# Transformer layer on eight cores: softmax division after the row sum moved behind a DRAM broadcast, weight casts issued one step ahead

## The chip, the cores and the metric

One Trainium2 chip. The same program runs on all 8 of its cores, each with its own rows of the result; the cores do not talk to each other. The metric is the device time in microseconds (us) of the slowest core. Engines are named as in the profile: PE is TensorE (matmul), PEld its weight loads, DVE is VectorE, ACT is ScalarE, POOL is GpSimd, SP is SyncE, which here only issues DMAs.

## The reference, cut to what matters

```python
# x: (2, 4096, 2048), float32
def attn(x):                       # 32 heads of 64 features
    q, k, v = x @ Wq + bq, x @ Wk + bk, x @ Wv + bv
    scores = einsum('bdsh,bdth->bdst', q, k) / sqrt(32)
    weights = softmax(scores, axis=-1)
    feats = einsum('bdst,bdth->bdsh', weights, v)
    return feats @ Wo + bo
def ffn(x):                        # hidden size 5632, integer weights
    return qlinear(silu(qlinear(x, wq_gate)) * qlinear(x, wq_up), wq_down)
x = x + attn(layernorm(x))
x = x + ffn(layernorm(x))
```

## The kernel before, in words

Core c takes batch c//4 and 1024 of its 4096 rows as queries; it computes K and V for all 4096 rows itself. Every step of the program is appended to one list with its engine, the semaphore counts it waits for and the one it raises (`st`, L173). Each engine then executes its own steps strictly in the order of the list, with no scheduler behind it. So the place of a step in the list is its place in its engine's queue, and a step that waits holds up all behind it on the same engine.

The stages, in order of time:

- **Projection** (L262 to L419), in two halves of 2048 rows. LayerNorm first (L263 to L314). Then for `w` in k, v (and q in the first half) and for each of 16 blocks `fo` of 128 output features: SP loads 1 MB of float32 weights into `wst` (L332, two buffers), ACT casts them to bf16 in `wbf` (L337, two buffers), PE does 64 matmuls of 128x512 (32 for q, L349), and ACT evacuates PSUM to `kev` or `qT` (L365, two evacuations, one for q). For k and q, ACT squares the result (L375, L413), and PE and DVE take turns over it in `_norms` (L233) to find a bound on the scores. For v, PE transposes `kev` in two groups of eight (L386), ACT copies each group to `vts` (L393), and POOL issues four DMAs to `vslab` in DRAM (L407). In ACT's queue the cast of block `fo` stands behind all the ACT work of block `fo-1`, and the first matmul of block `fo` waits for that cast.
- **Attention** (L467 to L582), 16 pairs of two heads, `p` and `h2`, head number `d = 2p + h2`. The K and V of a pair come by SP DMAs (`prefetch`, L488), issued two pairs ahead, when the last PE step of a pair is over. V has an extra column of ones, so row 64 of the result in PSUM is the softmax's row sum. A head has 32 chunks `c` of 128 keys. For each, PE computes the scores (two matmuls, L523, PSUM banks 0,1 or 2,3 in turn), ACT takes the exponential into `pt` (L540, 1024 columns), and PE multiplies by V (two matmuls, L551) and accumulates in banks 4,5 (h2=0) or 6,7 (h2=1). The scores of chunk c+2 are issued just ahead of the V product of chunk c.
- **End of a head** (L559 to L573): DVE takes the reciprocal of row 64, 1024 numbers in one partition, into `rcd`; PE copies it to 64 partitions by multiplying it with a column of ones (`ones64`, L563), into banks 2,3, the banks which chunk 1 of the next head needs; ACT copies that to `ebc` (L568); DVE multiplies the head's result by it and writes `featsT` (L570). The scores of chunk 0 of the next head stand behind the multiplication by ones in PE's queue; those of chunk 1 also wait for ACT's copy (`prev_eb`).
- **Output projection** (L586 to L631): a bias load on POOL and eight DVE additions that need it, then 512 matmuls.
- **FFN** (L636 to L790): 44 blocks of gate and up matmuls, and a down projection after every group of eight.

Of the kernel before, what the change touches and what calls it, by code (L numbers as in the profile page):

```python
# [6 lines left out]
F32 = mybir.dt.float32  # L7
# [3 lines left out]
ALU = mybir.AluOpType  # L11
# [21 lines left out]
def build(stop_after=99, debug=False, sub=99):  # L33
    nc = bass.Bass("TRN2", target_bir_lowering=False)
# [42 lines left out]

    identb = alloc("identb", [128, 128], BF16)
    identf = alloc("identf", [128, 128], F32)
    ones64 = alloc("ones64", [128, 64], F32)  # L80
    biasB = alloc("biasB", [128, NH], F32)
    bqs = alloc("bqs", [128, 16], F32)
    bks = alloc("bks", [128, 16], F32)
# [15 lines left out]
    lds2 = alloc("lds2", [128, 128], F32)  # L99
    P_END = off[0]  # L100
    assert P_END - PB <= 4096, P_END - PB
    R1 = PB + 4096
    R2 = R1 + 32768
    R3 = R2 + 32768
    SB_LIMIT = 229376
# [4 lines left out]
    featsT = alloc("featsT", [128, 16 * TO], BF16, at=R2)  # L110
# [16 lines left out]
          alloc("va1", [128, 32 * 2 * 128], BF16, at=FL + 49152)]  # L127
    pt = [alloc("pt0", [128, TO], BF16, at=FL + 65536),
          alloc("pt1", [128, TO], BF16, at=FL + 67584)]
    ebc = alloc("ebc", [128, TO], F32, at=FL + 69632)  # L130
    rcd = ebc[64:65, 0:TO]
    owst = alloc("owst", [128, 16 * 512], F32, at=FL)
    owbf = [alloc("owbf0", [128, 16 * 512], BF16, at=FL + 32768),
            alloc("owbf1", [128, 16 * 512], BF16, at=FL + 49152)]
# [12 lines left out]
    wdbB = alloc("wdbB", [128, 4 * D], BF16, at=FL + 49152)  # L147
    sdb = alloc("sdb", [128, D], F32, at=FL + 65536)
    gsil = alloc("gsil", [128, TO], BF16, at=FL + 73728)
    assert FL + 75776 <= SB_LIMIT  # L150

    PSA = nc.alloc_psum_tensor("PSA", [128, 4096], F32)

# [31 lines left out]

    for t_, val in ((identb[:, :], 0.0), (identf[:, :], 0.0), (ones64[:, :], 1.0),
                    (kmax[:, :], 0.0), (qmax[:, :], 0.0),
                    (epst[:, :], EPS), (n128[:, :], -128.0),
                    (ldst[:, :], 0.0), (lds2[:, :], 0.0)):
        st("gpsimd", lambda g, tt=t_, val=val: g.memset(tt, val), inc=gS)  # L190
# [70 lines left out]
    if stop_after >= 1:  # L261
        for h in (range(2) if sub >= 11 else []):  # L262
# [64 lines left out]
            for iw, w in enumerate(ws):  # L327
                wt, bcol, wscale = Wmap[w]
                ntq = 1 if w == "q" else 2
                for fo in range(16):  # L330
                    pg = cast_g.get((iw, fo - 2), cast_g.get((iw - 1, 14 + fo), 0))
                    ldw = st("sync", lambda e, wt=wt, fo=fo: e.dma_start(  # L332
                        out=wst[fo % 2].ap().rearrange("p (c x) -> p c x", x=128),
# [4 lines left out]
                        out=wbf[fo % 2][:, :], in_=wst[fo % 2][:, :]),  # L338
                        waits=[(dWp[fo % 2], ldw), (tS, mmg), (sS, sS.n)], inc=sS)
                    cast_g[(iw, fo)] = cg  # L340
                    for tq in range(ntq):
                        pb = 0 if tq == 0 else 2
                        ev_p = evac_g.get((iw, fo - 1, tq),
                                          evac_g.get((iw - 1, 15, tq), 0))
                        for fi in range(16):
                            for nh in range(2):
                                mvw = lnxT[:, fi * 2048 + tq * 1024 + nh * 512:
                                           fi * 2048 + tq * 1024 + (nh + 1) * 512]
                                st("tensor", lambda t, pb=pb, nh=nh, fo=fo, fi=fi, mvw=mvw: t.matmul(  # L349
                                    bkf(pb + nh), wbf[fo % 2][:, fi * 128:(fi + 1) * 128],  # L350
                                    mvw, start=(fi == 0), stop=(fi == 15)),
                                    waits=([(sS, cg), (vS, ln_done), (sS, ev_p)]
                                           if fi == 0 and nh == 0 else []),
                                    inc=tS if (fi == 15 and nh == 1) else None)
# [14 lines left out]
                        evac_g[(iw, fo, tq)] = ev  # L369
# [97 lines left out]
    if stop_after >= 2:  # L467
# [38 lines left out]
        prefetch(0)  # L506
        prefetch(1)
        fn_guard = {}
        prev_exp30 = 0
        prev_eb = 0  # L510
        prev_av = None
        for p in range(NP):
            need_dF = 160 * (p // 2 + 1)
            for h2 in range(2):
# [19 lines left out]
                for c in range(32):  # L534
# [21 lines left out]
                            waits=avw2 if qh == 0 else [],  # L556
                            inc=tS if qh == 1 else None)
                    av_cnt[c] = tS.n
                rc = st("vector", lambda v, acb=acb: v.reciprocal(  # L559
                    out=rcd, in_=PSA[64:65, acb * 512:(acb + 2) * 512]),  # L560
                    waits=[(tS, av_cnt[31]), (vS, vS.n)], inc=vS)
                for qh in range(2):
                    st("tensor", lambda t, qh=qh: t.matmul(  # L563
                        PSA[0:64, (2 + qh) * 512:(3 + qh) * 512], ones64[64:65, 0:64],
                        rcd[:, qh * 512:(qh + 1) * 512], start=True, stop=True),
                        waits=[(vS, rc), (sS, exp_cnt[31])] if qh == 0 else [],
                        inc=tS if qh == 1 else None)
                eb = st("scalar", lambda s: s.copy(out=ebc[0:64, :], in_=PSA[0:64, 1024:2048]),  # L568
                        waits=[(tS, tS.n), (sS, sS.n)], inc=sS)
                fg = st("vector", lambda v, p=p, h2=h2, acb=acb: v.tensor_tensor(  # L570
                    out=featsT[h2 * 64:(h2 + 1) * 64, p * 1024:(p + 1) * 1024],
                    in0=PSA[0:64, acb * 512:(acb + 2) * 512], in1=ebc[0:64, :],
                    op=ALU.mult), waits=[(sS, eb), (vS, vS.n)], inc=vS)  # L573
                fn_guard[(p + 1, h2)] = fg
                prev_exp30 = exp_cnt[30]
                prev_eb = eb
                prev_av = av_cnt
                if h2 == 1:
                    pair_end[p] = tS.n
# [310 lines left out]
```

How the kernel before makes its waits and increments, by code:

```python
def build(stop_after=99, debug=False, sub=99):  # L33
# [787 lines left out]
               waits=[(dB, S["dB"].n)], inc=dO, k=16)  # L821
        if stop_after >= 2 and stop_after < 4:
            st("sync", lambda e: e.dma_start(out=dbg["f"].ap(), in_=featsT[:, :]), inc=dO, k=16)
        if stop_after >= 3:
            for i in range(8):
                st("sync", lambda e, i=i: e.dma_start(
                    out=dbg["r1"][i * 128:(i + 1) * 128, :], in_=res[:, i * D:(i + 1) * D]),
                   inc=dO, k=16)
    final = dO.n
    st("sync", lambda e: e.wait_ge(dO.h, final))
    with nc.Block() as blk:
        for ename in ENGS:
# [1 line left out]
                def body(e):  # L836
                    for (en, fn, waits, incs) in steps:
                        if en != ename:
                            continue
                        for (h, v) in waits:
                            e.wait_ge(h, v)
                        inst = fn(e)
                        for (s_, k_) in incs:
                            inst.then_inc(s_.h, k_)
```

## Time and profile before

| what | value |
|---|---|
| median of the 2 runs of before | 5039.8 us (4981.63 and 5097.97) |
| the profiled execution: its time | 5000.85 us |
| its span, slowest core (7) | 4999.3 us |
| spans of all cores | 4968.2 to 4999.3 us |
| mean granted TensorE clock | 0.854 to 0.861 |
| PE busy | 3645.9 us (73%) |
| ACT busy | 1949.0 us (39%) |
| DVE busy | 910.3 us (18%) |
| POOL busy | 164.5 us (3%) |

The span runs from the first to the last instruction of the slowest core. The granted clock is a share of full speed: 1.00 is 2.4 GHz and 0.50 is 1.2 GHz. A row of the timeline reads: start in us, duration in us (of a whole group where several instructions are merged), engine, line, operation, output<-inputs, and in square brackets how long the engine had been idle before it and whose end released it. SPq and POOLq rows are the issue of DMAs, not their transfer.

### The profile page before, as it was taken

The page shows a single profiled execution, that of the slowest core. Times are in us where ns is not written, and L with a number is a line of the kernel's source. Part 1 is how long each engine was busy: PE and PEld are TensorE (multiplying, and loading weights), DVE is VectorE, ACT ScalarE, POOL GpSimd, SP SyncE. Part 2 cuts the span into 40 slices and gives each one's busy share as a digit, 9 for nine tenths or more (in the row PEclk, how much of TensorE's full clock was granted, in tenths as well). Part 3 has the DMA queues.
Part 4 walks back from the last instruction along what each step waited for, and adds up shares of the span by engine and source line. Part 5 has one row for each costly group of instructions (what it writes and reads, how often), then busy time and mean ns, then how long its engine had stood idle before and what let it go on. Part 6 is the DMA issues. An engine that isn't in the chain of part 4 may idle for free.

```text
span 4999.3 us, 44517 instructions; the slowest of 8 cores (4968.2 to 4999.3 us)
## 1 busy us (share of the span) xinstructions
PE 3645.9 (73%) x15365; PEld 1448.1 (29%) x15365; DVE 910.3 (18%) x1172; ACT 1949.0 (39%) x1658; POOL 164.5 (3%) x190
## 2 busy tenths in 40 slices
PE   2676677674466777747777777777775879999997
PEld 1232333221222333312222222222221334444443
DVE  4211000013311100001111111111112232223223
ACT  3222222223222222237677676767765231232121
POOL 0000011100000011120000000000000000000000
PEclk9877888876677788879888888888887979999999
DMA  3211222222211122240010001100011343453343
GB/s 127 76 59 64 63 64 64 72 72 88 102 63 63 51 64 65 57 105 17 17 34 17 17 17 28 24 17 17 17 17 72 114 142 122 149 202 127 125 153 127
DMA packets 257363, 361.58 MB, mean 72 GB/s; under 512 B 140578, under 2 KB 140672, under 8 KB 243072
## 3 DMA queue, kind: packets, MB, share of 16 engines
q1 hardware_dynamic: 245888, 322.99, 21.4%
q0 software_dynamic: 11264, 35.75, 2.3%
q8 instruction: 136, 2.23, 0.2%
q14 instruction: 75, 0.61, 0.0%
HBM read 316.76 MB, written 41.94 MB: 72 GB/s over the span
## 4 chain that ended last, share of the span: by engine, by line
PE 62%; ACT 18%; DVE 10%; issue 6%; DMA 2%; POOL 1%; ACTq 0%; DVEq 0%; SPq 0%; POOLq 0%
PE PSA L349 24%; ACT pt L540 11%; PE PSA L523 7%; PE PSA L773 6%; PE PSA L731 6%; PE PSA L741 6%; PE PSA L551 5%; DVE ebc L559 4%; PE PSA L563 2%; PE PSA L617 2%; PE PSA L237 2%; DVE scr L244 2%; ACT kev L365 1%; ACT vts L393 1%; ACT sqst L375 1%
## 5 line engine op out<-in xcount | busy, mean ns | idle before, releaser
L349 PE MATMUL PSA<-lnxT,wbf 128*128 128x512 bf16 x4608 | 1187.0, 425 | 112.0 <-ACT wbf L337 110.5
L540 ACT ACTIVATE pt<-PSA,biasB 128x1024 bf16<-128x1024 f32 x1024 | 1102.4, 1112 | 193.8 <-PE PSA L551 120.2
L523 PE MATMUL PSA<-qT,kp 128*128 128x512 bf16 x2048 | 652.9, 402 | 226.2 <-ACT pt L540 148.1
L349 PEld LDWEIGHTS PSA<-lnxT,wbf 128*128 128x128 bf16 x4608 | 490.1, 107 | 777.7 <-issue 375.7
L551 PE MATMUL PSA<-pt,va 128*128 128x512 bf16 x2048 | 623.9, 387 | 24.5 <-ACT pt L540 24.0
L559 DVE RECIPROCAL ebc<-PSA 1x1024 f32<-1x1024 f32 x32 | 209.8, 6555 | 1282.3 <-PE PSA L551 1282.3
L523 PEld LDWEIGHTS PSA<-qT,kp 128*128 128x128 bf16 x2048 | 135.7, 97 | 762.1 <-issue 761.7
L244 DVE TENSOR_REDUCE scr<-PSA 128x8 f32<-128x512 bf16 x160 | 110.7, 692 | 1278.6 <-PE PSA L237 1278.6
L237 PE MATMUL PSA<-identb,sqst 128*128 128x128 bf16 x640 | 87.1, 283 | 335.9 <-DVE kmax L252 149.5
L365 ACT ACTIVATE kev<-PSA,bks 128x1024 bf16<-128x1024 f32 x64 | 71.3, 1114 | 656.7 <-PE PSA L349 656.7
L731 PE MATMUL PSA<-ln2xT,wgb 128*128 128x512 bf16 x1408 | 313.0, 381 | 2.9 <-ACT wgb L709 2.9
L741 PE MATMUL PSA<-ln2xT,wub 128*128 128x512 bf16 x1408 | 311.1, 379 | 0.0
L551 PEld LDWEIGHTS PSA<-pt,va 128*128 128x128 bf16 x2048 | 196.8, 98 | 297.3 <-issue 81.6
L563 PE MATMUL PSA<-ebc,ones 1*64 1x512 f32 x128 | 116.5, 1062 | 223.4 <-DVE ebc L559 223.4
L365 ACT ACTIVATE kev<-PSA,bvs 128x1024 bf16<-128x1024 f32 x64 | 71.3, 1114 | 504.7 <-PE PSA L349 430.6
L749 ACT ACTIVATE gsil<-PSA,sgc 128x1024 bf16<-128x1024 f32 x44 | 49.0, 1114 | 503.6 <-PE PSA L731 503.5
L301 PE MATMUL PSA<-identb,lnst 128*128 128x128 bf16 x512 | 70.8, 302 | 200.1 <-ACT lnst L290 187.1
L773 PE MATMUL PSA<-wdbA,gub 128*128 128x512 bf16 x768 | 180.4, 381 | 11.8 <-DVE gub L755 11.8
L731 PEld LDWEIGHTS PSA<-ln2xT,wgb 128*128 128x128 bf16 x1408 | 138.2, 98 | 170.5 <-issue 5.6
L741 PEld LDWEIGHTS PSA<-ln2xT,wub 128*128 128x128 bf16 x1408 | 137.8, 98 | 166.2
L568 ACT COPY ebc<-PSA 64x1024 f32<-64x1024 f32 x32 | 32.2, 1006 | 368.4 <-PE PSA L563 368.4
L237 PEld LDWEIGHTS PSA<-identb,sqst 128*128 128x128 bf16 x640 | 51.9, 120 | 383.3 <-issue 383.3
(100 smaller groups left out, 2003.0 us busy)
## 6 DMA issues: line engine op xcount, KB each, us to landing
wdi<-wd SPq DMA_DIRECT2D x44, 1024.0 KB, 5.0
xst<-xb SPq DMA_DIRECT2D x32, 1024.0 KB, 5.3
kslab<-kev POOLq DMA_DIRECT2D x32, 512.0 KB, 2.9
vslab<-vts POOLq DMA_DIRECT2D x128, 128.0 KB, 4.4
kp<-kslab SPq DMA_DIRECT2D x32, 512.0 KB, 6.6
va<-vslab SPq DMA_DIRECT2D x128, 128.0 KB, 3.2
owst<-wo SPq DMA_DIRECT2D x4, 4096.0 KB, 13.8
res<-xb SPq DMA_DIRECT2D x8, 1024.0 KB, 19.4
```

What stands on the lines that cost most here:

```text
L237: st("tensor", lambda t, b4=b4, j=j, bank=bank, sqtile=sqtile: t.transpose(bkb(bank)[:, j * 128:(j + 1) * 128], sqtile[:, (b4 * 4 + j) * 1 ...
L244: st("vector", lambda v, bank=bank: v.reduce_sum(out=scr.ap().rearrange("p (a b) -> p a b", b=2)[:, 0:4, :], in_=bkb(bank)[:, 0:512].rearr ...
L349: st("tensor", lambda t, pb=pb, nh=nh, fo=fo, fi=fi, mvw=mvw: t.matmul(bkf(pb + nh), wbf[fo % 2][:, fi * 128:(fi + 1) * 128], mvw, start=( ...
L365: wscale=wscale: s.activation(out=dst, in_=bkf(pb, 2), func=AF.Identity, bias=bcol[:, fo:fo + 1], scale=wscale),
L523: st("tensor", lambda t, p=p, h2=h2, c=c, qh=qh: t.matmul(bkf((0 if c % 2 == 0 else 2) + qh), kp[p % 2][:, h2 * TB + c * 128: h2 * TB + (c ...
L540: e = st("scalar", lambda s, p=p, c=c, d=d: s.activation(out=pt[c % 2][:, :], in_=bkf(0 if c % 2 == 0 else 2, 2), func=AF.Exp, bias=biasB[ ...
L551: st("tensor", lambda t, p=p, h2=h2, c=c, qh=qh, acb=acb: t.matmul(PSA[:, (acb + qh) * 512:(acb + qh + 1) * 512], vav[p % 2][:, c, h2, 0:128],
L559: rc = st("vector", lambda v, acb=acb: v.reciprocal(out=rcd, in_=PSA[64:65, acb * 512:(acb + 2) * 512]), waits=[(tS, av_cnt[31]), (vS, vS. ...
L563: st("tensor", lambda t, qh=qh: t.matmul(PSA[0:64, (2 + qh) * 512:(3 + qh) * 512], ones64[64:65, 0:64], rcd[:, qh * 512:(qh + 1) * 512], s ...
L731: st("tensor", lambda t, fi=fi, nh=nh, hc=hc: t.matmul(bkf(nh), wgb[:, fi * 128:(fi + 1) * 128], ln2xT[:, fi * 1024 + nh * 512: fi * 1024 ...
L741: st("tensor", lambda t, fi=fi, nh=nh, hc=hc: t.matmul(bkf(2 + nh), wub[:, fi * 128:(fi + 1) * 128], ln2xT[:, fi * 1024 + nh * 512: fi * 1 ...
L773: wdbuf=wdbuf, wslot=wslot, last=(jj == len(grp) - 1): t.matmul(bkf(pb + nh), gub[:, jj * 1024 + qt * 128:jj * 1024 + (qt + 1) * 128], wdb ...
```

## The change

Two edits, and a third that follows from them.

**Casts.** Load and cast of a weight block become a helper, `ldcast`. It is called for block 0 before the loop, and inside the loop for block `fo+1` ahead of the matmuls of block `fo` (for block 0 of the next matrix when `fo` is 15).

**End of a head.** The reciprocal no longer reads PSUM, and PE no longer broadcasts. ACT copies row 64 to partition 0 of `nbc` (`dsb`), DVE copies the undivided result to `featsT` in bf16 and takes the reciprocal in place, POOL writes the 1024 reciprocals to DRAM (`dslab`) and reads them back to 64 partitions of `nbc`, and DVE multiplies `featsT` in SBUF. The next head's chunk 1 waits only for the last exponential.

**Memory.** `ones64` and its memset are gone, and the big buffers begin right behind the small ones: 512 bytes lower in each partition than before.

```diff
-    R1 = PB + 4096
+    R1 = ((P_END + 63) // 64) * 64
...
+                def ldcast(iw, fo, wt):
                     pg = cast_g.get((iw, fo - 2), cast_g.get((iw - 1, 14 + fo), 0))
                     ldw = st("sync", lambda e, wt=wt, fo=fo: e.dma_start(
...
                     cast_g[(iw, fo)] = cg
+
+                if (iw, 0) not in cast_g:
+                    ldcast(iw, 0, wt)
+                for fo in range(16):
+                    if fo + 1 < 16:
+                        ldcast(iw, fo + 1, wt)
+                    elif iw + 1 < len(ws):
+                        ldcast(iw + 1, 0, Wmap[ws[iw + 1]][0])
+                    cg = cast_g[(iw, fo)]
...
-                rc = st("vector", lambda v, acb=acb: v.reciprocal(
-                    out=rcd, in_=PSA[64:65, acb * 512:(acb + 2) * 512]),
+                cd = st("scalar", lambda s, acb=acb: s.copy(
+                    out=dsb, in_=PSA[64:65, acb * 512:(acb + 2) * 512]),
+                    waits=[(tS, av_cnt[31]), (sS, sS.n), (vS, nrm_g.get(d - 1, 0)),
+                           (dR, rsb_dma.get(d - 1, 0))],
+                    inc=sS)
+                fg = st("vector", ... v.tensor_copy(
+                    out=featsT[h2 * 64:(h2 + 1) * 64, p * 1024:(p + 1) * 1024],
+                    in_=PSA[0:64, acb * 512:(acb + 2) * 512]),
                     waits=[(tS, av_cnt[31]), (vS, vS.n)], inc=vS)
-                for qh in range(2):
-                    st("tensor", lambda t, qh=qh: t.matmul(
-                        PSA[0:64, (2 + qh) * 512:(3 + qh) * 512], ones64[64:65, 0:64],
-                        rcd[:, qh * 512:(qh + 1) * 512], start=True, stop=True),
-                        waits=[(vS, rc), (sS, exp_cnt[31])] if qh == 0 else [],
-                        inc=tS if qh == 1 else None)
-                eb = st("scalar", lambda s: s.copy(out=ebc[0:64, :], in_=PSA[0:64, 1024:2048]),
-                        waits=[(tS, tS.n), (sS, sS.n)], inc=sS)
-                fg = st("vector", lambda v, p=p, h2=h2, acb=acb: v.tensor_tensor(
+                fn_guard[(p + 1, h2)] = fg
+                rc = st("vector", lambda v: v.reciprocal(out=rsb, in_=dsb),
+                        waits=[(sS, cd), (vS, vS.n), (dR, rsb_dma.get(d - 1, 0))], inc=vS)
+                st("gpsimd", lambda g, d=d: g.dma_start(
+                    out=dslab[d].unsqueeze(0), in_=rsb),
+                    waits=[(vS, rc)], inc=dR, k=16)
+                rsb_dma[d] = dR.n
+                st("gpsimd", lambda g, d=d, h2=h2: g.dma_start(
+                    out=nbc[0][h2 * 64:(h2 + 1) * 64, :],
+                    in_=dslab[d].unsqueeze(0).partition_broadcast(64)),
+                    waits=[(dR, dR.n), (vS, nrm_g.get(d - 1, 0))], inc=dR, k=16)
+                ng_ = st("vector", ... v.tensor_tensor(
                     out=featsT[h2 * 64:(h2 + 1) * 64, p * 1024:(p + 1) * 1024],
-                    in0=PSA[0:64, acb * 512:(acb + 2) * 512], in1=ebc[0:64, :],
-                    op=ALU.mult), waits=[(sS, eb), (vS, vS.n)], inc=vS)
-                fn_guard[(p + 1, h2)] = fg
+                    in0=featsT[h2 * 64:(h2 + 1) * 64, p * 1024:(p + 1) * 1024],
+                    in1=nbc[0][h2 * 64:(h2 + 1) * 64, :], op=ALU.mult),
+                    waits=[(dR, bcd), (vS, fg), (vS, vS.n)], inc=vS)
+                nrm_g[d] = ng_
...
-                prev_eb = eb
+                prev_eb = exp_cnt[31]
```

How the instructions stand on the engines. ACT's queue at the start of the projection, before (L337 is the cast, L365 the evacuations of a block, L375 the square):

```order
L290 ACTIVATE lnst<-xst_70,negmr,rstd 128x2048
L337 CAST wbf_73<-wst_71 128x2048
L365 ACTIVATE kev<-PSA,bks 128x1024 x2
L375 ACTIVATE sqst<-kev 128x2048
L337 CAST wbf_74<-wst_72 128x2048
L365 ACTIVATE kev<-PSA,bks 128x1024 x2
```

The same place after (L339, L376 and L386 are the same three steps):

```order
L291 ACTIVATE lnst<-xst_69,negmr,rstd 128x2048
L339 CAST wbf_72<-wst_70 128x2048
L339 CAST wbf_73<-wst_71 128x2048
L376 ACTIVATE kev<-PSA,bks 128x1024 x2
L386 ACTIVATE sqst<-kev 128x2048
L339 CAST wbf_72<-wst_70 128x2048
L376 ACTIVATE kev<-PSA,bks 128x1024 x2
```

A second cast stands ahead of the first evacuation. From there on the pattern of the queue is the old one, but each cast belongs to the block after the one whose matmuls come next.

PE's queue around the end of head 0, before (L523 scores, L551 products with V, L563 the multiplication by ones):

```order
L551 MATMUL PSA<-pt_84,va_81 128x512 x2
L551 MATMUL PSA<-pt_83,va_81 128x512 x2
L551 MATMUL PSA<-pt_84,va_81 128x512 x2
L563 MATMUL PSA<-ebc,ones_45 64x512 x2
L523 MATMUL PSA<-qT,kp_79 128x512 x6
L551 MATMUL PSA<-pt_83,va_81 128x512 x2
```

PE's queue there after (L537 scores, L565 products with V):

```order
L565 MATMUL PSA<-pt_83,va_80 128x512 x2
L565 MATMUL PSA<-pt_82,va_80 128x512 x2
L565 MATMUL PSA<-pt_83,va_80 128x512 x2
L537 MATMUL PSA<-qT,kp_78 128x512 x6
L565 MATMUL PSA<-pt_82,va_80 128x512 x2
```

The next head's scores now follow the last product with V directly. ACT's queue there, after (L554 the exponential, L573 the copy of the row sum), has the copy where the copy from banks 2,3 (L568) stood:

```order
L554 ACTIVATE pt_82<-PSA,biasB 128x1024
L554 ACTIVATE pt_83<-PSA,biasB 128x1024
L573 COPY nbc_84<-PSA 1x1024
L554 ACTIVATE pt_82<-PSA,biasB 128x1024
```

DVE's queue per head, after, is three instructions (before: L559 reciprocal and L570 product):

```order
L580 CAST featsT<-PSA 64x1024
L585 RECIPROCAL nbc_84<-nbc_84 1x1024
L597 TENSOR_TENSOR featsT<-featsT,nbc_84 64x1024
```

and POOL's, which had nothing in this stage after its memsets:

```order
L588 DMA dslab<-nbc_84 16x1x64
L592 DMA nbc_84<-dslab 64x1024
```

## Rows read from the trace of the kernel before

**Rows 1.** The page's chain of work that ended last, by engine and by line

```profile
PE 62%; ACT 18%; DVE 10%; issue 6%; DMA 2%; POOL 1%; ACTq 0%; DVEq 0%; SPq 0%; POOLq 0%
PE PSA L349 24%; ACT pt L540 11%; PE PSA L523 7%; PE PSA L773 6%; PE PSA L731 6%; PE PSA L741 6%; PE PSA L551 5%; DVE ebc L559 4%; PE PSA L563 2%; PE PSA L617 2%; PE PSA L237 2%; DVE scr L244 2%; ACT kev L365 1%; ACT vts L393 1%; ACT sqst L375 1%
```

**Rows 2.** Who waited for whom: total us, times, longest us

```profile
DVE ebc L559 <- PE PSA L551: 1282.3, 32, 95.1
...
PE PSA L563 <- DVE ebc L559: 223.4, 32, 7.0
...
PE PSA L349 <- ACT wbf L337: 110.5, 31, 3.8
```

**Rows 3.** Timeline, the end of one head and the start of the next

```profile
3003.26 0.59 PE L551 MATMUL PSA<-pt,va 128*128 128x512 bf16 x2 [0.41 <-ACT pt L540]
3004.03 6.55 DVE L559 RECIPROCAL ebc<-PSA 1x1024 f32<-1x1024 f32 x1 [38.12 <-PE PSA L551]
...
3010.84 3.64 PE L563 MATMUL PSA<-ebc,ones 1*64 1x512 f32 x4 [6.98 <-DVE ebc L559]
...
3014.62 1.01 ACT L568 COPY ebc<-PSA 64x1024 f32<-64x1024 f32 x1 [11.51 <-PE PSA L563]
3015.60 1.11 ACT L540 ACTIVATE pt<-PSA,biasB 128x1024 bf16<-128x1024 f32 x1
3015.67 10.36 SPq L503 DMA_DIRECT2D va<-vslab  x8
...
3018.82 2.12 ACT L540 ACTIVATE pt<-PSA,biasB 128x1024 bf16<-128x1024 f32 x2 [0.76 <-PE PSA L551]
...
3021.20 2.12 ACT L540 ACTIVATE pt<-PSA,biasB 128x1024 bf16<-128x1024 f32 x2 [0.26 <-PE PSA L551]
```

**Rows 4.** All reciprocals (L559): duration min/median/max ns, first and last start us

```profile
L559 DVE RECIPROCAL ebc<-PSA x32: 6555/6555/6556, 2236.2 to 3826.3; 1x1024 f32<-1x1024 f32 x32
```

**Rows 5.** Busy us by engine in stretches there, granted clock, DMA share, GB/s

```profile
3004.00:3006.00 2.00, 0.00 (x0) 0.00 (x0) 1.97 (x1) 0.00 (x0) 0.00 (x0) 0.74 0.00 0
...
3016.00:3018.00 2.00, 1.93 (x5) 0.43 (x4) 1.02 (x1) 1.77 (x2) 0.00 (x0) 0.50 1.00 229
...
3026.00:3028.00 2.00, 1.65 (x8) 0.51 (x6) 0.00 (x0) 2.00 (x2) 0.00 (x0) 1.00 0.96 150
```

**Rows 6.** Timeline, the end of a v block in the projection (PE and ACT)

```profile
803.30 0.61 PE L386 MATMUL PSA<-identb,kev 128*128 128x128 bf16 x8 [1.68 <-ACT kev L365]
...
805.37 0.61 PE L386 MATMUL PSA<-identb,kev 128*128 128x128 bf16 x8 [1.46 <-ACT vts L393]
...
807.28 1.90 ACT L337 CAST wbf<-wst 128x2048 bf16<-128x2048 f32 x1
...
809.53 4.75 PE L349 MATMUL PSA<-lnxT,wbf 128*128 128x512 bf16 x12 [3.55 <-ACT wbf L337]
```

**Rows 7.** Busy us in half-microsecond stretches there; the column before DMA is the clock

```profile
806.50:807.00 0.50, 0.00 (x0) 0.00 (x0) 0.00 (x0) 0.50 (x1) 0.00 (x0) 0.79 0.00 0
...
813.50:814.00 0.50, 0.50 (x4) 0.19 (x2) 0.00 (x0) 0.00 (x0) 0.00 (x0) 0.88 1.08 217
```

**Rows 8.** DMA issues: KB each, median us from issue to landing

```profile
wst<-wv SPq DMA_DIRECT2D x32, 0.5 KB, 7.0
...
bbrow<-nrow POOLq DMA_DIRECT2D x1, 0.1 KB, 7.7
biasB<-bbrow POOLq DMA_DIRECT2D x1, 16.0 KB, 8.7
```

**Rows 9.** ACT's timeline, an evacuation of v held by a DMA

```profile
844.90 1.11 ACT L365 ACTIVATE kev<-PSA,bvs 128x1024 bf16<-128x1024 f32 x1 [11.83 <-DMA vslab<-vts]
```

**Rows 10.** Timeline, from the last head to the output projection

```profile
3838.08 1.22 DVE L570 TENSOR_TENSOR featsT<-PSA,ebc 64x1024 bf16<-64x1024 f32 x1 [5.21 <-ACT ebc L568]
...
3849.52 2.29 DVE L591 TENSOR_TENSOR res<-res,bob 128x2048 f32<-128x2048 f32 x1 [10.22 <-DMA bob<-bo]
...
3867.48 92.79 PE L617 MATMUL PSA<-owbf,featsT 128*128 128x512 bf16 x419 [30.72 <-DVE res L594]
```

**Rows 11.** The densest stretch, in the FFN: busy us by engine and clock

```profile
4100.00:4300.00 200.00, 198.10 (x919) 89.63 (x917) 56.65 (x37) 53.21 (x32) 0.00 (x0) 1.00 0.48 164
```

More of the change, by code:

```diff
@@ L55, in build @@
     bbrow = nc.dram_tensor("bbrow", [NH], F32)
+    dslab = nc.dram_tensor("dslab", [NH, TO], F32)
     dbg = {}
@@ L79, in build @@
     identf = alloc("identf", [128, 128], F32)
-    ones64 = alloc("ones64", [128, 64], F32)
     biasB = alloc("biasB", [128, NH], F32)
@@ L129, in build @@
           alloc("pt1", [128, TO], BF16, at=FL + 67584)]
-    ebc = alloc("ebc", [128, TO], F32, at=FL + 69632)
-    rcd = ebc[64:65, 0:TO]
+    nbc = [alloc("nbc0", [128, TO], F32, at=FL + 69632)]
+    dsb = nbc[0][0:1, :]
+    rsb = dsb
     owst = alloc("owst", [128, 16 * 512], F32, at=FL)
@@ L149, in build @@
     gsil = alloc("gsil", [128, TO], BF16, at=FL + 73728)
-    assert FL + 75776 <= SB_LIMIT
+    assert FL + 73728 <= SB_LIMIT - 32, (FL, SB_LIMIT)
     PSA = nc.alloc_psum_tensor("PSA", [128, 4096], F32)
@@ L184, in build @@
     vav = [t.ap().rearrange("p (c h f) -> p c h f", h=2, f=128) for t in va]
-    for t_, val in ((identb[:, :], 0.0), (identf[:, :], 0.0), (ones64[:, :], 1.0),
+    for t_, val in ((identb[:, :], 0.0), (identf[:, :], 0.0),
                     (kmax[:, :], 0.0), (qmax[:, :], 0.0),
@@ L329, in build @@
                 ntq = 1 if w == "q" else 2
-                for fo in range(16):
+                def ldcast(iw, fo, wt):
                     pg = cast_g.get((iw, fo - 2), cast_g.get((iw - 1, 14 + fo), 0))
@@ L508, in build @@
         fn_guard = {}
+        nrm_g = {}
+        rc_g = {}
+        rsb_dma = {}
         prev_exp30 = 0
@@ new lines, in build @@
+                fg = st("vector", lambda v, p=p, h2=h2, acb=acb: v.tensor_copy(
+                    out=featsT[h2 * 64:(h2 + 1) * 64, p * 1024:(p + 1) * 1024],
+                    in0=PSA[0:64, acb * 512:(acb + 2) * 512]) if False else v.tensor_copy(
+                    out=featsT[h2 * 64:(h2 + 1) * 64, p * 1024:(p + 1) * 1024],
+                    in_=PSA[0:64, acb * 512:(acb + 2) * 512]),
+                    waits=[(tS, av_cnt[31]), (vS, vS.n)], inc=vS)
+                fn_guard[(p + 1, h2)] = fg
@@ new lines, in build @@
+                rc = st("vector", lambda v: v.reciprocal(out=rsb, in_=dsb),
+                        waits=[(sS, cd), (vS, vS.n), (dR, rsb_dma.get(d - 1, 0))], inc=vS)
+                rc_g[d] = rc
+                st("gpsimd", lambda g, d=d: g.dma_start(
[6 more added lines that the diff above has]
+                    waits=[(dR, dR.n), (vS, nrm_g.get(d - 1, 0))], inc=dR, k=16)
@@ L571, in build @@
+                bcd = dR.n
+                ng_ = st("vector", lambda v, p=p, h2=h2, d=d: v.tensor_tensor(
                     out=featsT[h2 * 64:(h2 + 1) * 64, p * 1024:(p + 1) * 1024],
-                    in0=PSA[0:64, acb * 512:(acb + 2) * 512], in1=ebc[0:64, :],
-                    op=ALU.mult), waits=[(sS, eb), (vS, vS.n)], inc=vS)
-                fn_guard[(p + 1, h2)] = fg
+                    in0=featsT[h2 * 64:(h2 + 1) * 64, p * 1024:(p + 1) * 1024],
+                    in1=nbc[0][h2 * 64:(h2 + 1) * 64, :], op=ALU.mult),
+                    waits=[(dR, bcd), (vS, fg), (vS, vS.n)], inc=vS)
```

## The prediction

> **What bounds the kernel now.** I read the chain of waits first [rows 1]. It is led by PE (62%), with ACT 18% and DVE 10%; the projection's matmuls (L349) are its largest part, and the end-of-head steps stand in it openly: the reciprocal L559 with 4% and the multiplication by ones L563 with 2%. So no engine is the bound over the whole span; the kernel is a row of stages, and what counts in each is which wait ends last. The list of who waited for whom [rows 2] gives the three waits that the change touches. DVE's 1282 us ahead of its reciprocals is an idle engine and costs nothing. PE's 223.4 us for the reciprocal (32 times, 7.0 each) and its 110.5 us for the weight cast (31 times, 3.6 each) are idle time of the engine that leads the chain, so they are real. Then I read the timeline at both places.
>
> At the end of a head [rows 3], PE's last product with V starts at 3003.26. The reciprocal runs 3004.03 to 3010.58 on one partition, PE multiplies by ones for 3.64 us, ACT copies for 1.01, and the next head's first exponential starts at 3015.60. In these 11.57 us ACT and PE, the two engines that carry this stage, do nothing for the chunks. The reciprocals run from 2236.2 to 3826.3 us, 32 of them [rows 4]: a pitch of 1590.1/31 = 51.29 us per head, of which 51.29 - 11.57 = 39.72 run from a first exponential to the next row sum.
>
> At the end of a v block [rows 6], the last transposes end at 805.98. ACT copies them, and casts until 809.18 because the cast stands behind the copy; the next block's matmuls start at 809.53, after 3.55 us of idle PE. The k and q blocks show no such wait: rows 2 count 31 of them, all the v blocks but one, and in the other blocks the norms on PE and DVE outlast the cast.
>
> **The change part by part.**
>
> *Casts.* ACT's queue keeps its pattern; each cast sits where the old one sat but serves the block after the next matmuls. So matmuls find their weights ready and follow the last transposes directly: 31 x 3.55 = 110 us off the chain. What is late next is nothing on PE itself; the evacuation needs the matmuls, which just come 3.55 us sooner. The loads lose a step of lead: the load for a block is issued when the cast two blocks back is over, as before, but the cast that needs it now comes a block sooner. A v block takes 24 us and a load 7.0 us to land [rows 8], so that stays hidden. For k and q blocks I take zero.
>
> The clock goes with it. The granted clock in this gap falls from 1.00 to 0.50 (2.4 to 1.2 GHz) at about 806.8, that is 0.8 us after the transposes ended, and returns at about 813.6 [rows 7], so 4.1 us of matmuls from 809.53 on run at half rate and lose 2.05 us. With the change the matmuls start at 805.98, ahead of the fall. Whether it still falls, a little later or earlier, the trace of before can't show. Bounds: all of it comes back (31 x 2.05 = 64 us gained), or it falls sooner and the matmuls are cold for 5.2 us instead (as much as 0.6 us each lost, 18 us; a bound estimated by taking the cold time a quarter longer than in rows 7). I take 15 us gained, since the idle stretches that remain (1.68 and 1.46 us, [rows 6]) are those that the clock outlasted before.
>
> *End of a head.* ACT's new copy of the row sum starts where the reciprocal started and takes as long as the copy in rows 3, 1.01 us, since both are 1024 columns. Meanwhile PE does the next head's first scores, which no longer stand behind anything, and the first exponential follows: 1.01 us in place of 11.57, so 10.56 us saved per head. The trace of before shows no copy of one partition and none that reads a PSUM bank while DVE reads other partitions of it. Bounds: 1.01 us, or both reads one after the other, 1.01 + 1.22 (the DVE step of rows 3 in [rows 10]), which would cost 31 x 1.22 = 38 us. I take 1.01, the row of the same shape.
>
> The clock again: before, it falls about one us into the reciprocal (0.74 over 3004 to 3006) and stays at 0.50 into the next head [rows 5], so the first two chunks take 3018.82 - 3015.60 = 3.22 us where the following two take 3021.20 - 3018.82 = 2.38: 0.84 us more per head. After the change PE's longest rest there is from the end of two pairs of scores to the end of the first exponential, some 1.5 us. I take three quarters of the 0.84, between nothing and all of it: 0.63.
>
> So 31 boundaries x (10.56 + 0.63) = 347 us.
>
> *What moves off the path.* Per head, counted from the last product with V: DVE's cast of the result, 1.22 (the like of L570, [rows 10]), the reciprocal 6.55, both behind ACT's copy, so 7.85 with the hand-over; then two POOL DMAs in a row. The trace of before has the same pair once, the bias of the exponentials through `bbrow`: 7.7 and 8.7 us to landing [rows 8]. Then a product, 1.22. Sum: 7.85 + 7.7 + 8.7 + 1.2 = 25.5 us. The new pitch is 51.29 - 11.19 = 40.1 us. The next head's row-sum copy on ACT waits for that product, so there are 14.6 us of slack. The K and V prefetch, issued at every second boundary, runs the DMA engines at a share of 1.0 for about 12 us [rows 5]; it is over about 13 us after the boundary, when the first small DMA is five us old. Even 5 us more on it leaves 9. DVE is idle there otherwise, and POOL has nothing in its queue. If this cover went, ACT's queue would stop at the copy, and with it the exponentials.
>
> *The end of the stage.* After the last head nothing hides that chain: the bias load of the output projection waits for it, then DVE's additions, then PE's matmuls [rows 10]. Before, the result was ready 13.0 us after the last reciprocal began (3826.3 to 3839.3), now 25.5: 12.5 us lost. The two landings are the unknown in it; bounds are the old 7.7 + 8.7, and double that, 16 us more.
>
> On such DMAs the Trainium skill (DMA: Bandwidth & Descriptors, Anatomy of one DMA, SWDGE path) says that one costs 2.0 us plus its bytes over 436 GB/s. By that the pair would be an estimated 4.6 us in place of the trace's 16.4, and the end of the stage would lose about 1 us, not 12.5. The trace's two rows were measured from issue to landing on this chip, and decide.
>
> *Memory.* Shifting the buffers by 512 bytes and one memset less: zero.
>
> *Sum.* 4999.3 - 110 - 15 - 347 + 12.5 = 4539.8 us of span, and the profiled execution's time is 1.55 us above its span: 4541 us. That is against the profiled 5000.85; the median of the two runs shown, 5039.8, is 0.8% above it, since one of the two is 5097.97. A changed kernel timed in a like spread may read up to that much higher than my sum, and the range leaves room.
>
> **The rivals.**
>
> *The gain of the casts is given back.* An evacuation of v also waits for the DMAs to `vslab` of the block before: one started 11.83 us after its engine fell idle, released by that DMA [rows 9]. The matmuls come 3.55 us sooner, the DMAs don't, so this wait can grow. For it: the row. Against: PE has a second pair of banks to fill meanwhile, about 7 us. If it took all, the time would be 4541 + 125 = 4666.
>
> *The chain off the path is late.* If the landings take twice as long (32.8 us), the chain is 41.9 us, 1.8 us over the pitch: 31 x 1.8 = 56 us, with 16 more at the end: 4613. For it: the prefetch at half of the boundaries. Against: 14.6 us of slack.
>
> *Slower than before.* The same place, and one mechanism: the copy of the row sum on ACT, the stage's own engine, now waits for two DMAs through DRAM, and all exponentials stand behind it. It begins to cost when the two landings sum to over 16.4 + 14.6 = 31 us, and it eats the whole gain of 459 us when they reach 31 + 459/31 = 46 us; at 50 us it is 31 x 4 = 124 us slower than before, 5125. That needs three times the landings of rows 8, in every head.
>
> *The chip grants less clock to denser work.* The Trainium skill (TensorE: Matmul & The Clock Gate, Seeing it yourself) warns that dense matmuls on three or more cores of a die bring the clock down to 13/16 of full speed. In this trace the densest stretch, 200 us with PE busy for 198.1, is granted 1.00 [rows 11], on a chip where all eight cores run the same program, so the trace does not bear it out. Worked out as a mechanism of this kernel: the projection's matmuls are 24% of the chain [rows 1], 1200 us; were they a fifth slower, 240 us, the time would be 4541 + 240 = 4781, still faster than before.
>
> **How the numbers follow.** My forecast 0.80; casts given back 0.08; late chain 0.07; lower clock 0.03; slower than before 0.02. The low end is everything that the clock could give (49 more in the projection, 6 in the heads) and nothing at the end of the stage: about 4480. The high end adds the reads one after the other (38), a cold start of each head (20) and an earlier fall of the clock in the projection (33) to the sum, 4632, or the late chain, 4613: 4640. About two per cent is what a measurement of this kernel can tell from no change. All cases but the slower one lie more than 4% below before; for unforeseen cover I leave 0.03 to no difference, so faster 0.95, same 0.03, slower 0.02.
>
> **What would show each step right or wrong.** In the profile of after, PE's wait for the cast should be gone from the list of waits, and the matmuls of a v block should start within 0.2 us of the transposes. The pitch of the reciprocals should be 40 us, the first exponential should start about 1.1 us after the last product with V, and the clock should stay at 1.00 across most boundaries. The copy of the row sum should wait for PE, never for a DMA or DVE. The two POOL DMAs should land within about 16 us in sum. I am wrong if ACT waits at that copy for DVE, if the copy takes over 2 us, if the evacuations of v wait for `vslab` longer than PE's second pair of banks covers, or if the granted clock is lower in stretches that were at 1.00.

## The result, and the profile after

| what | before | after |
|---|---|---|
| median of all runs | 5162.58 us (4980.93 to 5429.05, 10 runs) | 4501.18 us (4491.18 to 4905.36, 11 runs) |
| fastest run | 4980.93 us | 4491.18 us |
| profiled execution: time, span | 5000.85, 4999.3 us | 4491.32, 4488.9 us |
| mean granted clock, by core | 0.854 to 0.861 | 0.906 to 0.909 |

The ratio is 0.902, with a 95% interval of 0.9007 to 0.9034. It compares undisturbed runs; in the others (6 of 10 before, 5 of 11 after) the cores of one die or of both were granted less clock (0.81 in parts of the traces kept of such runs) and took longer, so the medians of all runs, here and below, say little of the change. The forecast was 4541 us, range 4480 to 4640.

The waits that the change touches, in the kernel after (who waited for whom: us in total, times, longest us). L360 is the projection's matmul, L376 the evacuation, L573 the copy of the row sum, L588 and L592 the two POOL DMAs:

```profile
ACT kev L376 <- DMA vslab<-vts: 236.1, 28, 11.3
DVE featsT L597 <- DMA nbc<-dslab: 223.9, 32, 8.4
POOL nbc L592 <- DMA dslab<-nbc: 69.6, 32, 3.5
```

and the page's group of the projection's matmuls, which answers to [rows 2]:

```profile
L360 PE MATMUL PSA<-lnxT,wbf 128*128 128x512 bf16 x4608 | 1138.6, 413 | 1.5 <-DVE lnxT L310 1.5
```

PE no longer waits for a cast: its idle time before these matmuls is 1.5 us in all. It also no longer waits for DVE at a head's end. What is new is that DVE and POOL wait for DMAs. Between the heads no other engine waits for these two; only after the last head does the bias load of the output projection wait for DVE's product.

The timeline at the end of a head in the kernel after (core 1, its slowest), which answers to [rows 3]:

```profile
2750.95 0.59 PE L565 MATMUL PSA<-pt,va 128*128 128x512 bf16 x2 [0.41 <-ACT pt L554]
2751.39 1.02 PE L537 MATMUL PSA<-qT,kp 128*128 128x512 bf16 x4
...
2751.72 1.22 DVE L580 CAST featsT<-PSA 64x1024 bf16<-64x1024 f32 x1 [24.16 <-PE PSA L565]
2751.80 1.00 ACT L573 COPY nbc<-PSA 1x1024 f32<-1x1024 f32 x1 [0.99 <-PE PSA L565]
...
2752.83 2.12 ACT L554 ACTIVATE pt<-PSA,biasB 128x1024 bf16<-128x1024 f32 x2
2753.11 6.54 DVE L585 RECIPROCAL nbc<-nbc 1x1024 f32<-1x1024 f32 x1 [0.17 <-DVE featsT L580]
2754.09 0.59 PE L537 MATMUL PSA<-qT,kp 128*128 128x512 bf16 x2 [1.67 <-ACT pt L554]
...
2755.21 2.12 ACT L554 ACTIVATE pt<-PSA,biasB 128x1024 bf16<-128x1024 f32 x2 [0.26 <-PE PSA L565]
```

The four scores of the next head (L537) stand directly behind the last product with V; the copy takes 1.00 us with DVE reading the same bank beside it; the first exponential starts 1.03 us after the copy did, where it started 11.57 us after the reciprocal. From the first exponential pair to the second it is 2755.21 - 2752.83 = 2.38 us, the steady pace, with no cold start. The clock there, in stretches of 2 us (columns as in [rows 5]):

```profile
2750.00:2752.00 2.00, 1.59 (x7) 0.49 (x8) 0.28 (x1) 1.01 (x2) 0.00 (x0) 1.00 0.00 0
2752.00:2754.00 2.00, 0.41 (x2) 0.00 (x0) 1.83 (x2) 1.98 (x3) 0.00 (x0) 1.00 0.64 143
2754.00:2756.00 2.00, 1.91 (x8) 0.64 (x8) 2.00 (x1) 1.74 (x2) 0.00 (x0) 1.00 0.95 205
```

PE is busy for only 0.41 of the middle 2 us and the granted clock stays at 1.00. On this core it does not fall once from 2050 us to 3311 us: over all 31 boundaries between heads. It is low in the first 6 us of the stage, which begins at 2032 us after a wait of 54 us, and it falls again at 3311.5 us, behind the last head.

Where the time went is best read on one core. All three rows are of core 0: the first and the last row sum before (L559) and after (L573), and the last product of after (L597):

```profile
L559 DVE RECIPROCAL ebc<-PSA x32: 6555/6555/6556, 2213.1 to 3800.4; 1x1024 f32<-1x1024 f32 x32
```

```profile
L573 ACT COPY nbc<-PSA x32: 1004/1004/1005, 2067.3 to 3304.6; 1x1024 f32<-1x1024 f32 x32
L597 DVE TENSOR_TENSOR featsT<-featsT,nbc x32: 1216/1220/1224, 2081.4 to 3318.6; 64x1024 bf16<-64x1024 bf16 x32
```

Up to the first row sum 2213.1 - 2067.3 = 145.8 us are gained. From the first to the last it is 1587.3 before and 1237.3 after: 350.0 gained, a pitch of 39.91 us. The last result is ready 13.0 us after the last row sum before and 15.2 after (3318.6 + 1.2 - 3304.6): 2.2 lost. From there on the two differ by 1.8 us. Sum: 493.6 + 1.8 = 495.4, which is the difference of the core's spans, 4978.6 - 4483.2.

### The profile page after: what moved, and what is told of

Same layout as the page of the kernel before. It is cut to its first block, busy times and chain, and to the rows that moved or that the text cites. A ratio compares the mean times of both kernels' runs of the same rounds, so it can differ in the third digit from the quotient of the medians.

```text
span 4488.9 us, 44576 instructions; the slowest of 8 cores (4475.4 to 4488.9 us)
## 1 busy us (share of the span) xinstructions
PE 3417.2 (76%) x15237; PEld 1410.0 (31%) x15237; DVE 948.7 (21%) x1204; ACT 1938.1 (43%) x1658; POOL 196.8 (4%) x253
## 4 chain that ended last, share of the span: by engine, by line
PE 64%; ACT 19%; DVE 6%; issue 6%; DMA 2%; POOL 1%; ACTq 0%; DVEq 0%; SPq 0%; POOLq 0%
PE PSA L360 25%; ACT pt L554 13%; PE PSA L537 7%; PE PSA L801 7%; PE PSA L759 7%; PE PSA L769 7%; PE PSA L565 6%; PE PSA L645 3%; PE PSA L238 2%; DVE scr L245 2%; ACT kev L376 2%; ACT sqst L386 1%; DVE stat L273 1%; PE PSA L397 1%; DMA xst<-xb 1%
## 5 line engine op out<-in xcount | busy, mean ns | idle before, releaser
L554 ACT ACTIVATE pt<-PSA,biasB 128x1024 bf16<-128x1024 f32 x1024 | 1090.2, 1111 | 179.0 <-PE PSA L565 122.8
L360 PE MATMUL PSA<-lnxT,wbf 128*128 128x512 bf16 x4608 | 1138.6, 413 | 1.5 <-DVE lnxT L310 1.5
L537 PE MATMUL PSA<-qT,kp 128*128 128x512 bf16 x2048 | 603.2, 378 | 264.8 <-ACT pt L554 207.2
L360 PEld LDWEIGHTS PSA<-lnxT,wbf 128*128 128x128 bf16 x4608 | 481.0, 105 | 626.1 <-issue 174.5
L565 PE MATMUL PSA<-pt,va 128*128 128x512 bf16 x2048 | 608.5, 378 | 24.7 <-ACT pt L554 24.4
L537 PEld LDWEIGHTS PSA<-qT,kp 128*128 128x128 bf16 x2048 | 133.4, 96 | 721.6 <-issue 714.1
L376 ACT ACTIVATE kev<-PSA,bks 128x1024 bf16<-128x1024 f32 x64 | 71.3, 1114 | 653.0 <-PE PSA L360 653.0
L565 PEld LDWEIGHTS PSA<-pt,va 128*128 128x128 bf16 x2048 | 192.8, 96 | 284.7 <-issue 61.3
L376 ACT ACTIVATE kev<-PSA,bvs 128x1024 bf16<-128x1024 f32 x64 | 71.3, 1114 | 364.3 <-DMA vslab<-vts 236.1
L580 DVE CAST featsT<-PSA 64x1024 bf16<-64x1024 f32 x32 | 39.0, 1218 | 832.5 <-PE PSA L565 832.5
L585 DVE RECIPROCAL nbc<-nbc 1x1024 f32<-1x1024 f32 x32 | 209.3, 6541 | 6.0 <-DVE featsT L580 5.5
L811 DVE SCALAR_TENSOR_TENSOR res<-PSA,res 128x1024 f32<-128x1024 f32 x96 | 117.6, 1225 | 201.6 <-PE PSA L801 201.6
```

The lines of the kernel that those rows point to most:

```text
L376: wscale=wscale: s.activation(out=dst, in_=bkf(pb, 2), func=AF.Identity, bias=bcol[:, fo:fo + 1], scale=wscale),
L537: st("tensor", lambda t, p=p, h2=h2, c=c, qh=qh: t.matmul(bkf((0 if c % 2 == 0 else 2) + qh), kp[p % 2][:, h2 * TB + c * 128: h2 * TB + (c ...
L554: e = st("scalar", lambda s, p=p, c=c, d=d: s.activation(out=pt[c % 2][:, :], in_=bkf(0 if c % 2 == 0 else 2, 2), func=AF.Exp, bias=biasB[ ...
L565: st("tensor", lambda t, p=p, h2=h2, c=c, qh=qh, acb=acb: t.matmul(PSA[:, (acb + qh) * 512:(acb + qh + 1) * 512], vav[p % 2][:, c, h2, 0:128],
L585: rc = st("vector", lambda v: v.reciprocal(out=rsb, in_=dsb), waits=[(sS, cd), (vS, vS.n), (dR, rsb_dma.get(d - 1, 0))], inc=vS)
```

## The experiments

**Each edit alone.** The first kernel is before with `ldcast` and its calls, the second is before with the end-of-head part of the diff and the moved buffers. No line is new in either.

> Before, with the casts edit alone. If the projection's part of the gain is the wait and the clock (my theory after reading both traces), the first row sum comes 163 us sooner than before and the time is 163 us below before, about 4820 us, ratio 0.967. If the clock gained only the 15 us of the prediction, 125 us below before, about 4857 us, ratio 0.975. If the rest of the 163 us came from the end-of-head edit, 110 us or less.

Measured: ratio 0.9758 (0.9643 to 0.9872), fastest run 4839.98 us against 4981.15. The interval lies below 1, but it is too wide to tell 125 us from 163; the trace is sharper. Core 0 has its first row sum here:

```profile
L569 DVE RECIPROCAL ebc<-PSA x32: 6554/6555/6556, 2070.6 to 3658.2; 1x1024 f32<-1x1024 f32 x32
```

That is 142.5 us sooner than core 0 of before, at an unchanged pitch of 51.21. The fastest runs differ by 141 us. My expectation of 163 was too high because it came from core 7 of before's profile, whose first row sum (2236.2) was 23 us later than that of core 0.

> Before, with the end-of-head edit alone. Theory: pitch of the row sums 39.9 us in place of 51.3, so 353 us less, minus 3 at the end of the stage: 350 us below before, about 4632 us, ratio 0.930. The two edits add up: 163 + 350 = 513. Rival, that they share a part (fewer than 350 here because the clock or the DMA queues differ between the two): below 330 or above 370.

Measured: 4634.39 us, ratio 0.9302 (0.9275 to 0.9329). On core 0:

```profile
L563 ACT COPY nbc<-PSA x32: 1005/1005/1006, 2206.0 to 3443.3; 1x1024 f32<-1x1024 f32 x32
```

The pitch is 39.91 us, the same as with both edits. The fastest runs give 349 us for this edit and 141 for the casts, together 490; both edits together give 4980.93 - 4491.18 = 489.75. The two add up, to within the 1 us by which the fastest runs of one kernel differ. Core 0 has its first row sum here 7 us sooner than in before; that is within the spread of before's cores 0 to 5 (2205.8 to 2215.5 us). The moved buffers were not run apart from this edit.

**The clock's part in the casts edit.** Of 142 us only 110 are the wait. To see the rest by itself, this kernel leaves the wait where it is and takes PE's rest away, by matmuls whose result nobody reads:

```diff
+                        for z in range(14):
+                            st("tensor", lambda t: t.matmul(
+                                bkf(6), identb[:, :], lnxT[:, 0:512],
+                                start=True, stop=True))
                         vtd = sS.n
```

> Before, with 14 more matmuls of 128x512 (weights identb, result never read) behind the last transposes of every v block: 3.0 us of work in PE's idle 3.55 us ahead of the cast-bound matmuls. The idle time is not taken away, only PE's rest. Theory (the clock is a part of what the casts edit gains): the clock stays at 1.00 there, the 64 matmuls of a v block take about 13.9 us in place of 16.0, and the time falls by up to 31 x 2.05 = 64 us, to about 4920. Rival (the wait alone is the gain, the clock has no part or falls anyway): within 10 us of 4981; slower if the filler delays the matmuls.

Measured: 4945.05 us, ratio 0.9917 (0.9893 to 0.9941): faster by some 41 us, under 1% (the interval lies below 1), with more work and no wait less. PE's timeline shows both cases (L401 is the filler, L349 the block's matmuls):

```profile
617.12 5.54 PE L401 MATMUL PSA<-lnxT,identb 128*128 128x512 bf16 x14
622.49 13.98 PE L349 MATMUL PSA<-lnxT,wbf 128*128 128x512 bf16 x62
...
664.92 2.97 PE L401 MATMUL PSA<-lnxT,identb 128*128 128x512 bf16 x13
668.43 13.97 PE L349 MATMUL PSA<-lnxT,wbf 128*128 128x512 bf16 x63 [0.54 <-ACT wbf L337]
```

and the granted clock in the two fillers' stretches, 0.51 and 1.00 (the column after the busy times):

```profile
616.00:622.00 6.00, 5.69 (x20) 2.59 (x21) 0.00 (x0) 2.97 (x3) 2.93 (x4) 0.51 0.19 44
...
664.00:668.00 4.00, 3.58 (x21) 1.75 (x22) 0.00 (x0) 2.85 (x3) 0.89 (x1) 1.00 0.00 0
```

In both blocks the 64 matmuls take 13.98 us, not the 15.97 that they take behind an idle gap. In the first the clock had fallen already, the filler itself ran at half rate for 5.5 us and held the matmuls up by about 2 us. Of the 16 groups of fillers in the first half nine take over 4 us, and the pitch of the v blocks there is 22.6 us in place of 23.9: 1.3 us gained of the 2.05, which in 31 blocks is the 41 us. So the clock is a cause of its own, shown with the wait still there.

How often it still falls in after is in the same view of that kernel (L360):

```profile
668.53 13.98 PE L360 MATMUL PSA<-lnxT,wbf 128*128 128x512 bf16 x64
...
686.76 15.60 PE L360 MATMUL PSA<-lnxT,wbf 128*128 128x512 bf16 x64
```

Of fifteen v blocks from 589.70 us to 880.77 us, five run at 13.98 and ten between 15.2 and 16.4, and the pitch is 291.07/15 = 19.40 us where before it was 23.9. 3.55 of those 4.5 us are the wait, about 1.0 is the clock (15.98 us for the matmuls of a block before, 15.05 on average now): 32 us in all blocks, and with the 110 the 142 that were measured. In the second half six of sixteen blocks run at 13.98.

**How long do the two small DMAs take?** My 16.4 us came from [rows 8]. In after, the same kind of pair lands like this (DMA issues: KB each, median us from issue to landing):

```profile
nbc<-dslab POOLq DMA_DIRECT2D x32, 256.0 KB, 3.5
...
dslab<-nbc POOLq DMA_DIRECT2D x32, 4.0 KB, 1.6
...
bbrow<-nrow POOLq DMA_DIRECT2D x1, 0.1 KB, 8.4
biasB<-bbrow POOLq DMA_DIRECT2D x1, 16.0 KB, 8.3
```

A write 32 times larger (4096 bytes against 128) lands in 1.6 us and the tiny one takes 8.4, in one and the same execution. At that moment SP issues the loads of the residual, eight times 1 MB. The next kernel issues them later:

```diff
-                waits=kvw if i == 0 else [], inc=dRs, k=16)
+                waits=kvw + [(dB, bias_rdy)] if i == 0 else [], inc=dRs, k=16)
```

> Before, with the eight 1 MB loads of the residual issued only after the pair of small DMAs for the bias. Theory: that pair took 7.7 and 8.7 us to land because those 8 MB went through the same DMA engines at the same time; alone it lands like the pair of after, about 1.6 and 3.5 us. Rival: the pair is slow in itself (first POOL transfers after a rest, or 8-byte pieces), and stays at 7 us or more each. The whole time stays within 10 us of before in either case.

Measured, in the profile:

```profile
bbrow<-nrow POOLq DMA_DIRECT2D x1, 0.1 KB, 3.2
biasB<-bbrow POOLq DMA_DIRECT2D x1, 16.0 KB, 5.7
```

On this slowest core 16.4 us became 8.9. Over the eight cores the pair took 12.8 to 18.3 us in before and takes 5.2 to 9.6 us here, so the neighbours' 8 MB made up about half of it, and the rival that the pair is slow in itself is out. Most cores are still above the 5.1 us of the steady pair: four writes to `vslab` are issued within 4 us ahead of it in the same queue, and whether they are the rest was not tried. The three executions read 5171.64 to 5281.58 us; in the profiled one cores 0 to 3, at 0.860 like before, span 4968.6 to 4978.3 us, as in before.

**How much slack has the chain off the path?** After, with the two DMAs repeated in each head, five and three more times:

```diff
+                for _r in range(5):
+                    st("gpsimd", ... out=dslab[d].unsqueeze(0), in_=rsb),
+                        waits=[(dR, dR.n)], inc=dR, k=16)
+                    rsb_dma[d] = dR.n
+                    st("gpsimd", ... in_=dslab[d].unsqueeze(0).partition_broadcast(64)),
+                        waits=[(dR, dR.n)], inc=dR, k=16)
                 bcd = dR.n
```

> After, with the write and the read back of the reciprocals repeated five more times in each head. One pair costs 6.6 us in POOL's queue, so the chain off the path grows from 16.3 to about 49.5 us, 9.6 us over the pitch of 39.9. Theory (ACT's copy of the row sum waits for the product of the head before): the pitch becomes the chain, 49 to 51 us, the copy's wait is put down to DVE or DMA, and the time grows by some 300 us to about 4790. Rival (the chain is off the path whatever its length, or the wait sits elsewhere): pitch stays 39.9, and the time at 4491.

Measured: 4809.39 us, a single execution. All row-sum copies of its slowest core, with what ended the idle time before them, and one boundary:

```profile
L573 ACT COPY nbc<-PSA x32: 1005/1005/1006, 2071.7 to 3597.9; 1x1024 f32<-1x1024 f32 x32
...
  DVE featsT L606: 273.7, 31
```

```profile
2723.83 1.22 DVE L606 TENSOR_TENSOR featsT<-featsT,nbc 64x1024 bf16<-64x1024 bf16 x1 [42.76 <-DMA nbc<-dslab]
2725.15 1.22 DVE L580 CAST featsT<-PSA 64x1024 bf16<-64x1024 f32 x1
2725.19 1.00 ACT L573 COPY nbc<-PSA 1x1024 f32<-1x1024 f32 x1 [11.32 <-DVE featsT L606]
```

The pitch is 1526.2/31 = 49.2 us, the chain itself. ACT's copy now waits for DVE's product, 11.32 us here, and every exponential waits behind the copy. This is the mechanism of my slower rival, made real by length alone: 31 x 9.32 = 289 us in the pitch and 34 at the end of the stage (from the last copy to the last result 49.3 us in place of 15.3), less some 5 in the other stages, are the 318 between the two times. It is still faster than before.

> After, with three more round trips through DRAM in each head. From the run with five more, a round trip costs 6.0 us: the chain is 16.3 + 18 = 34 us, below the pitch of 39.9. Theory (slack to the full length of a head): pitch 39.9 to 40.0 and a time within 15 us of 4491. Rival (the chain costs in proportion to its length): 31 x 3/5 of what five more cost, some 180 us more.

Measured: 4597.72 us in the fastest of three. Cores 4 to 7 of it were granted 0.905 to 0.907, about as in after, and are the ones to read. Core 4:

```profile
L573 ACT COPY nbc<-PSA x32: 1005/1005/1006, 2066.7 to 3304.0; 1x1024 f32<-1x1024 f32 x32
its engine sat idle before it (us, times) until:
  PE PSA L565: 30.7, 31
```

The pitch is 39.91 us, and the copy waits for PE alone, 1.0 us a head as in after. These cores span 4501.1 to 4510.5 us, some 20 more than after, so my 15 us were too few: from the last copy to the last result it is 33.6 us in place of 15.3, the three round trips, which nothing hides there. From copy to result the chain is 33.2 to 36.5 us in this kernel, all of it covered, and 45.8 to 56.5 us in the one before, whose pitch grew to the chain's mean. So the cover ends between 36.5 and 45.8 us, where the pitch of 39.9 lies.

**What the projection still leaves.** The last two kernels go beyond the change. The first puts such fillers into all waits of PE there (14, 11 or 6 ahead of a block's first transposes, 6 between the groups) and takes no wait away:

> After, with such filler matmuls in every wait of PE in the projection: 14 (k), 11 (q) or 6 (v) ahead of the first transposes of a block and 6 between the groups. No wait is taken away. Theory: the clock never falls in the projection outside LayerNorm; a k or q block then saves the 5 us of cold matmuls at half rate, 2.6 us each, a v block the 1.0 us that it still loses: 48 x 2.6 + 32 x 1.0 = 157 us, to about 4335 us. Rival (what is granted sinks with denser work on all cores, or the fillers are in the way): 4491 or more.

Measured: 4352.31 us, ratio to before 0.8735 (0.8718 to 0.8753), mean granted clock 0.961. On core 0 the first row sum comes at 1924.1 us, 143 sooner than in after. The clock does not fall once between 560 and 800 us. Work that nobody needs made the kernel 3% faster than after.

The second gives PE real work in these waits. The norms and the transposes of a block become a list of pieces, and the loop over the next block's matmuls takes one at `fi` 8 and 14 of the block's first 32 matmuls (`tq` 0) and 4 and 10 of its second 32:

```diff
                         for fi in range(16):
+                            if pend and fi in ((8, 14) if tq == 0 else (4, 10)):
+                                pend.pop(0)()
                             for nh in range(2):
...
+                        if w != "k":
+                            kevg = kv_end.get((h, 0, 15), 0)
...
-                            _norms(sqst, 16, kmax, fo, sqg)
+                            pend.extend(_norms(sqst, 16, kmax, fo, sqg))
```

> After, with the norms (k, q) and the transposes (v) of a block moved in between the matmuls of the next block, so that PE never waits for ACT or DVE at a block's end. If PE's work is then the bound of the projection, a block takes 64 x 0.216 + 16 x 0.056 = 14.7 us (k from 26.5, v from 19.4) and 7.8 us for q (from 13.8): 32 x 11.8 + 32 x 4.7 + 16 x 6.0 = 624 us less, to about 3870 us. If weight loads (7 us landing, needed every 7.8 us in q) or the evacuations of v, which wait for vslab, bind instead, 3950 to 4200 us.

Measured: fastest run 3907.53 us, ratio to before 0.7844 (0.7825 to 0.7863). The projection's PE timeline is closed, a v block in 14.71 us (L404 is the transposes):

```profile
452.30 0.61 PE L404 MATMUL PSA<-identb,kev 128*128 128x128 bf16 x8
452.74 2.75 PE L365 MATMUL PSA<-lnxT,wbf 128*128 128x512 bf16 x12
455.33 0.61 PE L404 MATMUL PSA<-identb,kev 128*128 128x128 bf16 x8
455.78 11.39 PE L365 MATMUL PSA<-lnxT,wbf 128*128 128x512 bf16 x52
467.00 0.61 PE L404 MATMUL PSA<-identb,kev 128*128 128x128 bf16 x8
```

The first row sum comes at 1482.5 us on core 0, 585 us sooner than in after; I had expected 624. A wait of PE for q's evacuation is new, 22.2 us over 15 blocks; the other 17 us I did not trace. This version beats both kernels.

## Why the prediction was right or wrong, point by point

The direction and the mechanism held, both waits went as forecast, and 4541 to 5000.85 is 0.908, against 0.902. What failed are sizes in the sum: the time of the undisturbed runs, 4491, is 50 us under the forecast, near the low end of the range. (That end was given as 4480; by its own terms it is 4541 - 49 - 6 - 12.5, about 4473.) Four terms made the 50 us up, and the largest are the base, 20 us too high, and the clock's term in the projection, 15 us taken where 32 came.

- *The base.* This was the first step that failed: I made the sum against one profiled execution and its slowest core, 5000.85 us, where before's fastest takes 4980.93. 20 of the 50 us. That core's first row sum came 23 us later than core 0's, and 18 of them arose in the q blocks: from the first matmul of the first of these 16 blocks to that of the last, core 7 takes 223.9 us (953.17 to 1177.07) and core 0 205.6 (954.74 to 1160.37). The profile shows why. On cores 6 and 7, and on no other core of it, the granted clock there is 0.81, neither of the two levels seen elsewhere, in fourteen stretches between 976 and 1193 us, 132 us in all. One of them, on core 7, with PE busy throughout:

```profile
1016.00:1021.00 5.00, 5.00 (x21) 2.07 (x19) 0.00 (x0) 0.00 (x0) 0.00 (x0) 0.81 0.25 92
```

  The high base also made me look for 163 us in the casts edit where there were 142. The room that I left upward for the spread of the runs was beside the point, since the spread is as wide in before: its median of ten runs is 5162.58.
- *Casts, the wait:* 110 us predicted, 110 found, with nothing on PE in its place.
- *Casts, the clock:* 15 us taken, about 32 measured, within my bounds of -18 and 64. The size was off. A third of the blocks keep the clock, and the others lose less than before; I had no row for how often.
- *The end of a head:* 10.56 + 0.63 a head predicted, 11.3 measured (51.21 - 39.91). The copy takes 1.00 us and DVE's cast beside it 1.22, so ACT and DVE reading one bank at a time cost nothing here. Of the clock's 0.84 us I took three quarters and all of it came; in all boundaries 350 us in place of 347: 3 us more.
- *The end of the stage:* 12.5 us predicted, 2.2 measured: 10 us. The term rested on landings of 7.7 and 8.7 us, which belong to a moment in which the queues are full; in this stage the median landings are 1.6 and 3.5. The Trainium skill's rule (DMA: Bandwidth & Descriptors, Anatomy of one DMA, SWDGE path), 2.0 us plus the bytes, gave 4.6 for the pair against 5.1 measured; I set the row above it, and the row was of another situation.

All four errors have one sign, hence 50 us: 20 + 17 + 3 + 10.

The rivals. *Casts given back:* the wait that I named did grow, from 74 to 236 us on ACT, and cost PE nothing: its idle time before the matmuls is 1.5 us in all. *Late chain* and *slower than before:* not in this kernel, whose chain from copy to result is about 16 us of a pitch of 39.9. Their common mechanism is shown at 49 us; at what length a kernel gets slower than before was not tried. *Lower clock for denser work:* the mean rose, from 0.860 to 0.908, and to 0.961 with fillers in every gap, and no core of after's profile shows the level 0.81. But my ground against this rival, that the trace of before does not bear it out, was a misreading: I looked at one stretch at 1.00 and missed the 132 us at 0.81 on cores 6 and 7. What brings that level on is open; core 0 ran the same program in the same execution without it.

## What to carry to other kernels

When the steps at the end of an iteration feed only its own result, give the next iteration's first work nothing to wait for but the last read of its buffers, and let the rest run on idle engines, even through DRAM: it is free until its length reaches the iteration's, and then it costs its full excess each time. When a queue is written by hand, look at what each engine waits for at a block's end and move that work into the next block's loop; here that was worth more than the change itself (584 us against 490). Take a duration from a row only together with what else was moving at that moment, and a base time from several cores, not from the slowest one of one execution.

## What was not expected of the hardware

In this projection a gap in PE's work costs twice, once as idle time and once as matmuls at 1.2 GHz after it: filling gaps with useless matmuls, with every wait left in place, made before 0.8% and after 3% faster. The clock fell at every head end of before, and at none of the 31 boundaries of after, where PE still rests for 1.67 us (on seven of its eight cores; core 2 shows one fall). Two cores of one die were granted 0.81 for 132 us of before's profile while the other six, on the same program, were not. The landing time of a small DMA varied from 1.6 us to 11.1 us (the write of 128 bytes in the kernel with five more round trips), with the load of the other queues and not with its size.
